# Attentive GRU stage on one core: one half of the keys and query summed in PSUM, two scans for the candidate's input and the new state

## The reference, cut to what matters

```python
def step(h, x_t):
    combined = jnp.concatenate([broadcast(h), enc_hiddens], axis=2)      # B, C, 2*128
    score = jnp.tanh(combined @ W_att) @ V_att[:, 0]                     # B, C
    attn = jax.nn.softmax(score, axis=-1)
    context = jnp.einsum('bs,bsh->bh', attn, enc_hiddens)
    gz, gr, gh = jnp.split(jnp.concatenate([x_t, context], 1) @ Wi + b, 3, axis=1)
    rz, rr, rh = jnp.split(h @ Uh, 3, axis=1)
    z, r = sigmoid(gz + rz), sigmoid(gr + rr)
    hh = jnp.tanh(gh + r * rh)
    return z * h + (1.0 - z) * hh
```

## Time and profile before

| | |
|---|---|
| median of 3 runs | 5423.73 us (5413.26 to 5431.53) |
| span of the profiled execution, first to last instruction | 5413.8 us |
| recurrent stage in it | about 424 to 1935 us |
| mean granted clock of TensorE, whole program | 0.918 |

### The profile page before, as it was taken

The page is one execution under the profiler, slowest core; times in us unless marked ns, Lnnn a source line. Parts: engine busy times, 40 slices in busy tenths (PEclk is TensorE's granted clock), DMA queues, the critical chain, the costliest instruction groups (busy, mean ns, idle before and its releaser), DMA issues. The chain is left out here.

```text
span 5413.8 us, 111310 instructions
## 1 busy us (share of the span) xinstructions
PE 4614.7 (85%) x45206; PEld 3112.5 (57%) x45501; DVE 2884.4 (53%) x9511; ACT 2082.3 (38%) x4120; POOL 576.5 (11%) x1302
## 2 busy tenths in 40 slices
PE   5489999999999965889989889899778979788784
PEld 3357777777777753555555555555444756566463
DVE  6634555555555535777766677666455224433433
ACT  2223333333333312665665666566433322212221
POOL 3300111111111112111111111111000000000000
PEclk8789999999999976999999999999889989878786
DMA  0000000000000011000000000000010010000000
GB/s 26 23 18 2 2 2 2 2 2 2 2 2 2 2 61 54 4 4 6 7 6 4 4 9 4 6 1 1 1 40 1 1 44 1 1 1 1 1 1 9
DMA packets 32272, 49.22 MB, mean 9 GB/s; under 512 B 8244, under 2 KB 23638, under 8 KB 31136
## 3 DMA queue, kind: packets, MB, share of 16 engines
q1 hardware_dynamic: 28448, 38.27, 2.2%
q10 hardware_dynamic: 2304, 2.11, 0.1%
q0 software_dynamic: 1024, 1.78, 0.1%
HBM read 37.72 MB, written 4.19 MB: 8 GB/s over the span
## 5 line engine op out<-in xcount | busy, mean ns | idle before, releaser
L2299 DVE TENSOR_REDUCE l_m<-psum 128x2 bf16<-128x512 f32 x768 | 503.8, 692 | 148.8 <-PE psum L1904 146.5
L2175 ACT ACTIVATE l_probs<-psum,l_mcol 128x1024 f32<-128x1024 f32 x384 | 406.3, 1109 | 159.2 <-PE psum L1942 159.2
L1184 PE MATMUL psum<-g_gx,ident 128*128 128x128 f32 x1536 | 416.0, 389 | 18.0
L1173 PE MATMUL psum<-g_still,ident_bf 128*128 128x256 bf16 (+3 forms) x1551 | 391.5, 281 | 1.7 <-PEq L58 1.7
L1904 PE MATMUL psum<-l_kb,l_qmb 32*128 32x256 bf16 x1536 | 295.4, 273 | 56.1 <-DVE l_m L2299 52.4
L1252 ACT ACTIVATE g_th<-g_pre 128x256 f32<-128x256 f32 x512 | 191.7, 417 | 314.3 <-DVE g_pre L1285 314.3
L1184 PEld LDWEIGHTS psum<-g_gx,ident 128*128 128x128 f32 x1536 | 279.4, 195 | 12.8
L1942 PE MATMUL psum<-l_qm,l_keys 32*128 32x256 f32 x3072 | 265.1, 418 | 13.3 <-issue 13.3
L2186 ACT COPY l_heads_out<-psum 128x256 f32<-128x256 f32 (+1 forms) x292 | 130.0, 445 | 369.8 <-PE psum L1968 186.3
L1285 DVE TENSOR_TENSOR g_pre<-g_encp,psum 128x256 f32<-128x256 f32 x512 | 192.8, 418 | 132.9 <-PE psum L1202 122.4
L2299 DVE TENSOR_REDUCE l_cm<-psum 128x4 bf16<-128x256 f32 x400 | 166.0, 427 | 179.8 <-PE psum L1904 179.6
(11 more groups left out here) (567 smaller groups left out, 9761.9 us busy)
## 6 DMA issues: line engine op xcount, KB each, us to landing
s_w<-in_S_w SPq DMA_DIRECT2D x16, 256.0 KB, 5.0
f_w<-in_F_w SPq DMA_DIRECT2D x2, 2048.0 KB, 12.5
l_wf<-in_L_W SPq DMA_DIRECT2D x6, 576.0 KB, 3.8
l_w<-in_L_W SPq DMA_DIRECT2D x1, 3072.0 KB, 10.6
l_nw<-in_L_nw SPq DMA_DIRECT2D x1, 2304.0 KB, 8.0
l_wc<-in_L_W SPq DMA_DIRECT2D x6, 384.0 KB, 3.0
h_w<-in_H_W ACTq DMA_DIRECT2D x16, 129.0 KB, 3.0
h_w<-in_H_W SPq DMA_DIRECT2D x16, 129.0 KB, 3.0
```

The costliest lines, as they stand in the source:

```text
L1173: pe.matmul(psum[:, bank, 0:cols], cst["ident_bf"][:], still[:, 0:cols], start=True, stop=True)
L1184: pe.matmul(psum[:, bank, 0:P], cst["ident"][:], repeated(gx(gate, s)), start=True, stop=False)
L2175: act.activation(probs[:, u % 2, chunk, :].rearrange("p (g n) -> p g n", g=GROUP), psum[:, 0:GROUP, S * chunk:S * chunk + S], ACT.Exp, bia ...
L2299: dve.tensor_reduce(place, psum[:, c.bank(("max", u, g)), 0:x.tiles * x.width] .rearrange("p (t k) -> p t k", t=x.tiles), AX.X, ALU.min)\
```

## The change

- The state `h` becomes [128, 2 buffers, 8, 2]; the state proper is the odd element of each pair, so its columns are 2 elements apart. The query and all hidden parts are computed from the state; the products with `zh` and `part` are gone, and with them `wa_half`.
- For the odd batches (`i` = 1) keys and query are summed in PSUM, bank 7: `keys_part`, an identity matmul over 256 columns, is issued one step ahead behind the scores, and `query_part`, W_att times the state's odd batches, each column repeated 64 times, behind the query. ScalarE reads this sum directly. The even batches keep their sum on VectorE.
- The candidate's sum in PSUM is over pairs: the even element holds half of the hidden part (`uh_half`, one matmul over 128 columns that fills even and odd), the odd one that plus input and context. The input's share lies in `GXC`, [128, 8, 256, 2], with zeros at the even places, zeroed on GpSimd in the setup. A scan with factors (0, tr) gives tr times the even one plus the odd one. It replaces L1303 and L1306.
- The new state is a scan as well: factors (0, (1-tz)/2), addends (candidate, (tz+1)h/2). GpSimd halves the state into `half` and stores it.
- All three input parts of the next step are issued at the end of the step, ahead of the query. The matmul of the candidate's hidden part stands behind the turn (L1226), that of the reset gate between query and scores, that of the update gate behind `keys_part`.
- One `keep_busy` a step is left. The outer loop, which ran once, is gone and the slices are fixed.

```diff
-STEPS_A_PASS = 256
+REPEATS = 16
...
-GX = sb("gx", [P, 3, B, S])
+GX, GXC = sb("gx", [P, 2, B, S]), sb("gxc", [P, B, S, 2])
...
+h0, half = sb("h0", [P, B]), sb("half", [P, B])
+h = sb("h", [P, 2, B, 2])
+uh_half = sb("uh_half", [P, D])
...
+pre, th = sb("pre", [P, PAIRS, C]), sb("th", [P, 2, PAIRS, C])
...
-wa_half = sb("wa_half", [P, D])
...
+tz = sb("tz", [P, B])
+reset, u = sb("reset", [P, B, 2]), sb("u", [P, B, 2])
+decay, addend = sb("decay", [P, B, 2]), sb("addend", [P, B, 2])
...
+        pool.memset(GXC[:], 0.0).then_inc(sig["shares_cleared"], 1)
...
+            dst = GX[:, i, 2 * p:2 * p + 2, :] if i < 2 else GXC[:, 2 * p:2 * p + 2, :, 1]
+            if n == 2:
+                act.wait_ge(sig["shares_cleared"], 1)
...
+        dve.memset(reset[:], 0.0)
+        dve.memset(decay[:], 0.0)
...
-        dve.tensor_scalar(wa_half[:], wa[:, 0, :], 0.5, None, ALU.mult)
+        dve.tensor_copy(h[:, 0, :, 1], h0[:])
+        dve.tensor_scalar(half[:], h0[:], 0.5, None, ALU.mult)
+        dve.tensor_scalar(uh_half[:], uh[:, 2, :], 0.5, None, ALU.mult)
...
-                    pe.wait_ge(sig["kept_part_ready"], s)
-                    pe.matmul(psum[:, 0, 0:P], wa_half[:], repeated(zh[:]), start=True, stop=False)
-                    pe.wait_ge(sig["new_part_ready"], s)
-                    pe.matmul(psum[:, 0, 0:B], wa[:, 0, :], part[:], start=False, stop=True)\
-                        .then_inc(sig["query_ready"], 1)
-                    keep_busy(3, 256)
-                    pe.wait_ge(sig["state_ready"], s)
-                pe.matmul(psum[:, 7, 0:P], uh[:, 2, :], repeated(hs), start=True, stop=True)\
-                  .then_inc(sig["state_products_ready"], 1)
-                if s >= 1:
-                    pe.wait_ge(sig["tanh_z_ready"], s)
-                input_part(0, 4, s)
-                if s >= 1:
-                    pe.wait_ge(sig["candidate_input_ready"], s)
-                input_part(2, 6, s)
...
-                turn_part(1, 6, "gate_h_ready")
-                keep_busy(3, 192)
-                pe.wait_ge(sig["context_z_taken"], s + 1)
-                turn_part(2, 4, "gate_z_ready")
-                keep_busy(3, 512)
-                if s + 1 < STEPS_A_PASS:
-                    pe.wait_ge(sig["tanh_r_ready"], s + 1)
-                    input_part(1, 5, s + 1)
-                    keep_busy(3, 256)
...
+    KEYS = 7
+    candidate = psum[:, 6, 0:2 * B].rearrange("p (b two) -> p b two", two=2)
...
+        def paired(cols):
+            return cols.unsqueeze(1).to_broadcast([P, REPEATS // 2, B, 2])
+        def candidate_input(s):
+            pe.matmul(psum[:, 6, 0:P], cst["ident"][:], paired(GXC[:, :, s, :]), start=True, stop=False)
+        def keys_part():
+            pe.matmul(psum[:, KEYS, 0:PAIRS * C], cst["ident"][:], encp[:, 1, :, :].rearrange("p b s -> p (b s)"),
+                      start=True, stop=False)
+        def query_part(hs):
+            pe.matmul(psum[:, KEYS, 0:PAIRS * C], wa[:, 0, :],
+                      hs[:, 1::2].unsqueeze(2).to_broadcast([P, PAIRS, C]), start=False, stop=True)\
+                .then_inc(sig["keyed_query_ready"], 1)
...
+        keep_busy(3, 512, 18)
+        input_part(1, 5, 0)
+        input_part(0, 4, 0)
+        candidate_input(0)
+        keys_part()
+        for s in range(S):
+            hs = h[:, s % 2, :, 1]
+            if s:
+                pe.wait_ge(sig["state_ready"], s)
+            pe.matmul(psum[:, 0, 0:B], wa[:, 0, :], hs, start=True, stop=True).then_inc(sig["query_ready"], 1)
+            query_part(hs)
+            pe.matmul(psum[:, 5, 0:P], uh[:, 1, :], repeated(hs), start=False, stop=False)
+            pe.wait_ge(sig["tanh_ready"], 2 * s + 1)
+            score_rows(0)
+            pe.wait_ge(sig["tanh_ready"], 2 * s + 2)
+            score_rows(1).then_inc(sig["scores_ready"], 1)
+            if s + 1 < S:
+                keys_part()
+            pe.matmul(psum[:, 4, 0:P], uh[:, 0, :], repeated(hs), start=False, stop=False)
...
+            pe.matmul(psum[:, 6, 0:P], uh_half[:], paired(hs.unsqueeze(2).to_broadcast([P, B, 2])), start=False, stop=False)
...
+            if s + 1 < S:
+                keep_busy(3, 320)
+                pe.wait_ge(sig["tanh_r_ready"], s + 1)
+                input_part(1, 5, s + 1)
+                pe.wait_ge(sig["tanh_z_ready"], s + 1)
+                input_part(0, 4, s + 1)
+                pe.wait_ge(sig["candidate_input_ready"], s + 1)
+                candidate_input(s + 1)
...
+            act.wait_ge(sig["tanh_input_ready"], s + 1)
+            act.activation(th[:, 0, :, :], pre[:], ACT.Tanh).then_inc(sig["tanh_ready"], 1)
+            act.wait_ge(sig["keyed_query_ready"], s + 1)
+            act.activation(th[:, 1, :, :], psum[:, KEYS, 0:PAIRS * C].rearrange("p (b s) -> p b s", s=C), ACT.Tanh)\
+                .then_inc(sig["tanh_ready"], 1)
...
+            act.activation(reset[:, :, 1], psum[:, 5, 0:B], ACT.Tanh, scale=0.5).then_inc(sig["tanh_r_ready"], 1)
+            act.wait_ge(sig["gate_z_ready"], s + 1)
+            act.activation(tz[:], psum[:, 4, 0:B], ACT.Tanh, scale=0.5).then_inc(sig["tanh_z_ready"], 1)
+            act.wait_ge(sig["candidate_input_ready"], s + 1)
+            act.activation(addend[:, :, 0], u[:, :, 1], ACT.Tanh).then_inc(sig["candidate_ready"], 1)
...
-                pool.tensor_scalar(kept[:], zh[:], 0.5, None, ALU.mult).then_inc(sig["kept_halved"], 1)
-                pool.wait_ge(sig["kept_halved"], s + 1)
-                pool.wait_ge(sig["new_part_ready"], s + 1)
-                pool.tensor_tensor(new, kept[:], part[:], ALU.add).then_inc(sig["state_ready"], 1)
-                pool.wait_ge(sig["state_ready"], s + 1)
-                pool.tensor_copy(HT[:, :, ds(group * STEPS_A_PASS + s, 1)], new.unsqueeze(2))
...
+            new = h[:, (s + 1) % 2, :, 1]
+            pool.wait_ge(sig["state_ready"], s + 1)
+            pool.tensor_scalar(half[:], new, 0.5, None, ALU.mult).then_inc(sig["state_halved"], 1)
+            pool.tensor_copy(HT[:, :, s:s + 1], new.unsqueeze(2)).then_inc(sig["state_stored"], 1)
...
-                dve.scalar_tensor_tensor(u[:], tr[:], 1.0, psum[:, 7, 0:B], ALU.add, ALU.mult).then_inc(sig["reset_ready"], 1)
-                dve.wait_ge(sig["gate_h_ready"], s + 1)
-                dve.wait_ge(sig["reset_ready"], s + 1)
-                dve.scalar_tensor_tensor(u2[:], u[:], 0.5, psum[:, 6, 0:B], ALU.mult, ALU.add)\
-                    .then_inc(sig["candidate_input_ready"], 1)
-                dve.wait_ge(sig["tanh_z_ready"], s + 1)
-                if s >= 1:
-                    dve.wait_ge(sig["state_ready"], s)
-                dve.scalar_tensor_tensor(zh[:], tz[:], 1.0, h[:, s % 2, :], ALU.add, ALU.mult)\
-                    .then_inc(sig["kept_part_ready"], 1)
-                steps.after(dve.tensor_scalar(omz[:], tz[:], -0.5, 0.5, ALU.mult, ALU.add))
-                dve.wait_ge(sig["candidate_ready"], s + 1)
-                dve.tensor_tensor(part[:], omz[:], cand[:], ALU.mult).then_inc(sig["new_part_ready"], 1)
...
+            dve.wait_ge(sig["query_ready"], s + 1)
+            dve.tensor_tensor(pre[:], encp[:, 0, :, :], psum[:, 0, 0:B:2].unsqueeze(2).to_broadcast([P, PAIRS, C]), ALU.add)\
+                .then_inc(sig["tanh_input_ready"], 1)
...
+            dve.wait_ge(sig["tanh_r_ready"], s + 1)
+            dve.wait_ge(sig["gate_h_ready"], s + 1)
+            dve.tensor_tensor_scan(u[:].rearrange("p b two -> p (b two)"), reset[:].rearrange("p b two -> p (b two)"),
+                                   candidate.rearrange("p b two -> p (b two)"), 0.0, ALU.mult, ALU.add)\
+                .then_inc(sig["candidate_input_ready"], 1)
+            dve.wait_ge(sig["tanh_z_ready"], s + 1)
+            if s:
+                dve.wait_ge(sig["state_halved"], s)
+            dve.scalar_tensor_tensor(addend[:, :, 1], tz[:], 1.0, half[:], ALU.add, ALU.mult)
+            steps.after(dve.tensor_scalar(decay[:, :, 1], tz[:], -0.5, 0.5, ALU.mult, ALU.add))
+            dve.wait_ge(sig["candidate_ready"], s + 1)
+            if s:
+                dve.wait_ge(sig["state_stored"], s)
+            dve.tensor_tensor_scan(h[:, (s + 1) % 2, :, :].rearrange("p b two -> p (b two)"),
+                                   decay[:].rearrange("p b two -> p (b two)"),
+                                   addend[:].rearrange("p b two -> p (b two)"), 0.0, ALU.mult, ALU.add)\
+                .then_inc(sig["state_ready"], 1)
```

More of the change, by code:

```diff
@@ L1049, in attentive_gru @@
         z, zT = sb("z", [P, TILES, D]), sb("zT", [P, TILES * P])
-        GX = sb("gx", [P, 3, B, S])
+        GX, GXC = sb("gx", [P, 2, B, S]), sb("gxc", [P, B, S, 2])
         HT = sb("ht", [P, B, S])
         encp = sb("encp", [P, 2, PAIRS, C])
-        h = sb("h", [P, 2, B])
-        pre, th = sb("pre", [P, 2, PAIRS, C]), sb("th", [P, 2, PAIRS, C])
+        h0, half = sb("h0", [P, B]), sb("half", [P, B])
+        h = sb("h", [P, 2, B, 2])
+        uh_half = sb("uh_half", [P, D])
```

(13 more changed lines are left out.)

162 lines of the change are left out of this document (65 added, 97 removed).

## The result

| | before | after |
|---|---|---|
| median of 8 runs, us | 5418.74 (5397.71 to 5431.53) | 5455.81 (5436.31 to 5462.04) |
| after to before | | 1.006, interval 1.004 to 1.0079 |
| profiled execution, span, us | 5413.8 | 5457.3 |

The changed kernel is 37 us slower, where +39 was forecast. First the page of the kernel after: busy time of the engines and the granted clock in 40 slices, to be held against the earlier trace rows.

What follows compares the result with a forecast made beforehand. The prediction took each recurrent step as one serial chain, with TensorE's queue holding it: 0.03 us (front) plus 0.124 (end) is 0.154 a step, times 255, +39 us on the 5423.7 median, so 5463 us, range 5435 to 5495.

Steps and rivals of the forecast that it cites:

- First sum, tanh, scores: Start of a step: second tanh starts 0.31 us behind the first and lasts 0.38; the exponential ends 0.10 sooner.
- Front: Step up to the context weights' load: TensorE's added work cancels the earlier scores, leaving it 0.03 us later.
- End: From context weights to query: the state waits 0.17 us for TensorE's input parts, making the query 0.124 later.
- The sum: Whole step: 0.03 plus 0.124 gives 0.154 us a step, times 255, +39 us.
- Scans: Two VectorE scans at the step's end: 0.19 us each, bounds 0.167 and 0.34; up to 0.26 each costs nothing.
- The third wait at 0.16: Last scan, from candidate to new state: a third semaphore wait makes the delay 0.16 us in all, against 0.10.
- the first fell: Rival: reads 8 bytes apart go at the strided rate in one to three parts, 5517 to 5624 us; chance 0.13.
- The second fell: Rival: TensorE never holds the chain; front keeps 0.10, end keeps 0.04, 5388 us; chance 0.20.
- The third fell: Rival: fixed addresses bring the input parts to 0.11 us, no change, 5421 us; chance 0.12.
- The fourth: Rival: fewer busy matmuls drop TensorE to 1.2 GHz in the stage, 2.3 us a step, 6050 us; chance 0.05.

Runs made afterwards that it cites:

- e7: The kernel before with the input's shares stored token by token, so a step's columns lie together: 5409.95 us, 0.9987 to before.
- e6: Changed kernel with e4 and e2 joined, keys part replacing the busy matmul, candidate's hidden part ahead of the exponential: 5362.62 us, 0.99 to before.
- e11: e6 with the first scan undone into a product and a sum on VectorE: 5375.34 us, 0.9925 to before.
- e2: Changed kernel with the update gate's input part moved from the step's end to behind the reset gate's hidden part: 5396.66 us, 0.9979 to before.
- e3: Changed kernel with two more VectorE instructions a step, results unread, delaying the new state: 5444.6 us, 1.0073 to before.
- e5: Changed kernel with both sums back on VectorE, without keys part and query part: 5970.53 us, 1.1031 to before.
- e9: e8 with four busy matmuls a step, two behind the query and two in the tail: 5369.96 us, 0.992 to before.
- e12: e6 with the second scan, for the new state, undone into a product and a sum: 5401.25 us, 0.9979 to before.
- e8: e6 with both sums on VectorE and the busy matmul of 320 columns back in the tail: 5862.49 us, 1.083 to before.
- e4: Changed kernel with the input's shares stored token by token, so a step's columns are contiguous: 5393.09 us, 0.9973 to before.
- e10: e5 with four busy matmuls a step, two behind the query and two behind the scores: 5443.64 us, 1.0065 to before.

## Why the prediction was right

The sign, the size and the mechanism held. By its own steps:

- **First sum, tanh, scores.** The second tanh was to start 0.31 behind the first and last 0.38; it starts 0.32 behind and lasts 0.365. The scores were to come 0.10 sooner; the exponential came 0.13 sooner. The prediction moved the second half's load and left the way from there to the minimum as it was, but that way is 0.03 shorter too, as in e7.
- **Front.** The keys part behind the scores was to take the gain back, leaving 0.01, and the candidate's hidden part to make it 0.03 later. It took back 0.09 (to -0.04) and then the rest: 0.00. The term was 0.03 too high. Both waits show in the timeline, and e6 removes both.
- **End.** The state was to be ready about 2.45 after the context weights begin: 6.03-3.57=2.46. TensorE was to hold it by 0.17: it does by 0.20. The end costs 0.173 instead of 0.124. This is the term that was mis-sized: the four strided passes took 0.86, not 0.84; the second pass of the candidate's input part began 0.13 behind the first, not 0.11; from the query's load to the sum it took 0.43, where the prediction's numbers leave 0.41 (8.16+0.124-7.87). Read from rows rounded to 0.01, these three are the 0.05 that the end came out too long.
- **The sum.** 0.154 forecast, 0.173 measured, so +44 us in the stage of the profiled execution, where +39 was forecast. The +37 of the medians carries the spread of the runs, and the two errors of opposite sign, 0.03 and 0.05, are part of why it came so near.
- **Scans.** Taken as 0.19: 0.192 and 0.186 to 0.19.
- **A rule that a later run refuted.** The third wait at 0.16 changed nothing in the sum, since the update gate's path set the end, but it was wrong and broke the expectation of e11.

The rivals: the first fell, since reads 8 bytes apart go at 0.11 a pass (272 ns for L1237) and those of pairs at 0.13, far from the strided 0.22. The second fell with e2 and e3. The third fell: L1184 still takes 391 ns. The fourth did not come true in the changed kernel, which keeps 1.00, but it is near: taking out keys part and query part brings it (e5), at +2.07 a step, close to the 2.3 that the prediction gave.

**Where the gain of the change went.** With a free queue, the sum in PSUM is worth 0.064 a step (e9 against e6) and the first scan 0.052 (e11). The 0.181 of e12 is no gain over the kernel before. There the query was summed in PSUM from the kept and the new part, so the sum that makes the state stood beside the chain and only one product of 0.17 (L1315) stood in it. From the end of the update gate's tanh to the end of the last VectorE instruction ahead of the query it is 0.50 in e7, the kernel before with the same columns, and 0.51 in e6 (medians over the stage). So the two scans together brought nothing there. e6 leads e7 by 0.129 a step: about 0.06 from the sum in PSUM, 0.04 because the context weights load 0.05 behind the copy and not 0.09, and 0.03 because the update gate's tanh comes sooner after the context weights.

The changed kernel had the first and the third of these gains too, and the 0.066 of e7, and lost more to the order of TensorE's queue. It moved two slow input parts from under the sums and tanh, where their slow reads cost 0.066 (e7), to just ahead of the new state (0.20), and put the keys part just ahead of the exponential (0.085) and the candidate's hidden part just ahead of the context (0.08). These three are 0.365, and e6, which removes them and computes all the same, is 0.368 a step faster than the changed kernel.

What stays open is what in e5 and e8 let the clock fall. In the last 10 us that e8's table shows wholly at 1.00, TensorE was busy for 8.59 of 10 us; the changed kernel had 13.92 of 16, nearly the same share, when its stage began, and stayed at 1.00, as the row below shows. So these busy shares don't tell the two apart.

```profile
428.00:444.00 16.00, 13.92 (x125) 9.90 (x125) 3.41 (x15) 3.69 (x12) 0.40 (x2) 1.00 0.01 2
```

## What to carry to other kernels

When work is moved on an in-order engine, price the place as well as the work: ask which result comes next there and how far behind the queue is when it arrives; the update gate's input part cost 0.20 us ahead of the new state and nothing that shows under a tanh (e2). A load of weights with no releaser named, or starting later than about 0.05 behind its operand, is the mark of such a queue. Before moving anything, look at how the moved instruction reads memory: laying the eight columns of a step side by side (e4) gave the same 0.20 a step as moving one input part (e2), since either clears the queue before the new state comes. And before a new instruction is priced against the work that it replaces, ask which part of that work stood on the chain: the state's sum did not.

## What was not expected of the hardware

- TensorE stayed at its 1.2 GHz level for a whole stage of 2000 us while the table showed it busy for 1822 of 1900 us (e5). Its instructions are longer at the lower clock, so the share looks higher (in e8 8.59 of 10 us at 1.00 and 9.73 at 0.50): a high busy share is no sign of a full clock, and the granted clock has to be read. The Trainium skill (TensorE: Matmul & The Clock Gate, "What's actually happening") calls the throttled state the default one, which activity releases; no run here shows which activity counts. Four busy matmuls of 512 columns a step brought the full clock back (e9, e10), and with the keys part and query part in the step (e6) it held without any.
- A tanh over 256 elements took 365 ns from PSUM and 416 ns from SBUF (the two activations of the front above: 0.36 and 0.42).
- Pairs 2 KB apart (L1190 after) cost nearly what contiguous data cost: 281 ns in the mean against 274 in e4, where the sixteen elements lie together. The distance itself does little harm; single elements 1 KB apart do (391 ns, L1184).
